# A gated recurrence with its input projection: weights loaded to all 128 partitions first, x turned in columns of four, the preamble in a new order

## The chip, the core and the metric

One core of a Trainium2 chip. The time is that of one execution on the device, in microseconds (us). TensorE is called PE here as in the profile, VectorE DVE, ScalarE ACT, GpSimd POOL; SP is the engine that only issues DMAs in this kernel. "ACTq" and "SPq" in a row are the queues from which ACT and SP issue DMAs.

## What is computed

A recurrence over 512 time steps with 512 units for a batch of 32, its inputs projected by three matrices W, its condition by three matrices C, its state by three matrices U; the input is added to the states at the end. Everything is float32.

```python
vz = video @ C_z + b_z;  vr = video @ C_r + b_r;  vh = video @ C + b       # video: (32, 512)
xz = seq @ W_z;  xr = seq @ W_r;  xh = seq @ W                             # seq = x: (32, 512, 512)
def step(h, xs):
    xzt, xrt, xht = xs
    z = sigmoid(xzt + h @ U_z + vz)
    r = sigmoid(xrt + h @ U_r + vr)
    hh = tanh(xht + r * h @ U + vh)
    h_new = (1.0 - z) * h + z * hh
    return (h_new, h_new)
result = x + all h_new, in order of time
```

## The kernel before

**Layout.** The batch has 32 rows, the partitions are 128, so a row vector of 512 numbers is laid out in J = 4 parts of 32 partitions with N = 128 columns each: partition 32 j + b holds columns 128 j to 128 j + 127 of batch row b. `part(j)` is a part's partitions, `cols(c)` a run of 128 columns. DVE's transpose turns each 32 x 32 block by itself. After it, partition 32 j + s, column 32 q + b holds number 128 j + 32 q + s of row b, and the contraction runs in Q = 4 passes q over 128 partitions. A weight matrix must have the same order of rows: partition 32 j + s, pass q holds row 128 j + 32 q + s. `load_weights` makes it so with one load for each part of 32 partitions, four to a matrix (`rows = source.rearrange("(j q s) e -> j s q e", ...)`). Parts 0 and 2 are issued by SP, 1 and 3 by ACT (`BY_QUEUE`).

**Split products.** The projections of x and the products with U_r and U_z are made of float16 parts. For this each matrix has its largest magnitude taken on DVE (`top_of_w`, line 529), summed over the partitions on PE (`total_w`, line 285), turned into a power of two on DVE (`scale_of_w`, lines 535 to 539), and split into a high half on ACT (`high_w`, line 407) and a rest on DVE (`rest_of_w`, line 546). W_r and W_z share a scale, W_h has its own, U_z and U_r share one. x goes the same way in sets of four time steps: sum of magnitudes on ACT (`sum_x`, line 382), total on PE (`total_x`, line 285), power on DVE (`power_x`, `least_x`, `up_x`), whole and high values on ACT (lines 385 and 388), rest on POOL (line 210), and at last `turn_x` (line 514), one DVE transpose for each time step, of 128 four-byte words that each hold a high and a low float16.

**Preamble.** SP and ACT issue the loads in the order in which `block` lists them: W_r, W_z, the first block of x (8 time steps), W_h, the condition, U_z, U_r, the biases, C_r, C_z, C_h, U_h, three more blocks of x. ACT waits for x before it issues its share of the C matrices and U_h. PE's order has the base products (line 255, the condition by C) behind all totals; DVE's has the bases (`bases`, lines 561 and 564) behind the rest of W_h and ahead of the rest of U_r. The first step can begin when the rests of U_r and U_z are made and x is projected for it.

**A step.** PE: the reset product h by U_r (line 303), the update product h by U_z (312), a quarter of the projection of a later time step (276), the candidate product (266), the other three quarters of the projection. DVE and ACT between them: gate_r (ACT, 432), reset and its transpose (DVE, 637 and 639), the seed of the next step's gates (518), `turn_x` for three steps ahead (514), gate_c (ACT, 441), taken (661), the new state (665), its transpose h_t (669), its high half h_hi (ACT, 428) and its rest h_lo (DVE, 611). The order within each engine is written out by hand; semaphores tie the engines together. Input blocks of 8 steps are loaded four blocks ahead.

## Time and profile before

| | |
|---|---|
| median of 3 runs | 2236.66 us (2235.65 to 2237.01) |
| profiled execution | 2234.19 us |
| its span, first to last instruction | 2232.4 us |
| PE busy | 2179.1 us (98%) |
| DVE busy | 1751.8 us (78%) |
| ACT busy | 1326.2 us (59%) |
| mean granted clock of PE | 0.999 |

The span is that of the instructions, the execution's time has a little around it. Busy time of PE is that of pipelined instructions and no measure of how well it is used. The page divides the span by engine, by line and by slices, and follows the chain that ended last; the trace can be asked for single instructions in a stretch, for groups by line and shape, and for what moved on the DMA engines in a stretch.

### The profile page before, as it was taken

The page shows a single profiled execution, that of the slowest core. Times are in us where ns is not written, and L with a number is a line of the kernel's source. Part 1 is how long each engine was busy: PE and PEld are TensorE (multiplying, and loading weights), DVE is VectorE, ACT ScalarE, POOL GpSimd, SP SyncE. Part 2 cuts the span into 40 slices and gives each one's busy share as a digit, 9 for nine tenths or more (in the row PEclk, how much of TensorE's full clock was granted, in tenths as well). Part 3 has the DMA queues.
Part 4 walks back from the last instruction along what each step waited for, and adds up shares of the span by engine and source line. Part 5 has one row for each costly group of instructions (what it writes and reads, how often), then busy time and mean ns, then how long its engine had stood idle before and what let it go on. Part 6 is the DMA issues. An engine that isn't in the chain of part 4 may idle for free.

```text
span 2232.4 us, 238869 instructions
## 1 busy us (share of the span) xinstructions
PE 2179.1 (98%) x107827; PEld 1805.7 (81%) x107827; DVE 1751.8 (78%) x8225; ACT 1326.2 (59%) x4623; POOL 689.1 (31%) x1546
## 2 busy tenths in 40 slices
PE   1899999999999999999999999999999999999999
PEld 1788888888888888888888888888888888888888
DVE  4678877877777787787777778778777777877876
ACT  3566666666666665666666566566666656656664
POOL 0233333333333333333333333333333333333332
PEclk9999999999999999999999999999999999999999
DMA  9101101101101101111111011011011011011000
GB/s 209 24 20 38 38 19 38 38 19 38 38 19 38 38 19 38 33 25 38 26 32 38 19 38 38 20 38 38 19 38 38 19 38 38 19 39 36 21 19 19
DMA packets 145138, 78.20 MB, mean 35 GB/s; under 512 B 8789, under 2 KB 140373, under 8 KB 144981
## 3 DMA queue, kind: packets, MB, share of 16 engines
q1 hardware_dynamic: 142388, 72.12, 13.4%
q10 hardware_dynamic: 2592, 4.72, 1.0%
q14 instruction: 150, 1.22, 0.2%
q8 instruction: 8, 0.13, 0.0%
HBM read 43.25 MB, written 33.55 MB: 34 GB/s over the span
## 4 chain that ended last, share of the span: by engine, by line
PE 97%; SPq 2%; DMA 1%; issue 0%; DVE 0%; ACT 0%; DVEq 0%
PE p_bank L276 45%; PE c_bank L266 21%; PE banks L303 16%; PE banks L312 15%; SPq L146 1%; DMA c_w<-in_L_cond_C_dram 1%; SPq L164 0%; PE p_bank L285 0%; DVE uz_lo L546 0%; DVE ur_lo L546 0%; SPq L154 0%; SPq L160 0%; PE c_bank L255 0%; DVE reset L637 0%; DVE h_lo L611 0%
## 5 line engine op out<-in xcount | busy, mean ns | idle before, releaser
L276 PE MATMUL p_bank<-w_hi,x_t 128*32 128x384 f16 x16480 | 1188.3, 326 | 0.0
L276 PE MATMUL p_bank<-w_lo,x_t 128*32 128x384 f16 x8240 | 706.9, 326 | 0.0
L276 PEld LDWEIGHTS p_bank<-w_hi,x_t 128*32 128x32 f16 x16480 | 470.2, 97 | 150.2 <-issue 1.5
L266 PEld LDWEIGHTS c_bank<-u,reset_t 128*32 128x32 f32 x32768 | 482.2, 110 | 96.9 <-DVE reset_t L639 95.0
L266 PE MATMUL c_bank<-u,reset_t 128*32 128x64 f32 x32768 | 551.8, 219 | 2.2 <-issue 2.2
L237 POOL TENSOR_TENSOR result<-x_nat,state 128x128 f32<-128x128 f32 x512 | 234.1, 457 | 989.2 <-DVE h_lo L611 987.4
L432 ACT ACTIVATE gate_r<-banks,gates_down 128x64 f32<-128x64 f32 x1024 | 265.6, 310 | 355.0 <-PE banks L303 341.9
L441 ACT ACTIVATE gate_c<-c_bank 128x64 f32<-128x64 f32 x1024 | 228.4, 223 | 288.5 <-PE c_bank L266 288.3
L223 POOL TENSOR_TENSOR kept<-keep,state 128x128 f32<-128x128 f32 x512 | 236.8, 463 | 520.7 <-ACT keep L435 520.7
L637 DVE TENSOR_TENSOR reset<-gate_r,state 128x64 f32<-128x64 f32 x1024 | 208.7, 204 | 205.3 <-ACT gate_r L432 199.1
L428 ACT ACTIVATE h_hi<-h_t 128x64 f16<-128x64 f32 x1024 | 260.8, 255 | 150.2 <-DVE h_t L669 83.2
L303 PE MATMUL banks<-ur_hi,h_hi 128*32 128x128 f16 x8192 | 300.5, 219 | 3.4 <-ACT h_hi L428 3.4
L303 PE MATMUL banks<-ur_hi,h_lo 128*32 128x128 f16 x8192 | 301.4, 221 | 0.0
L303 PE MATMUL banks<-ur_lo,h_hi 128*32 128x128 f16 x8192 | 300.4, 219 | 0.2 <-issue 0.2
L611 DVE SCALAR_TENSOR_TENSOR h_lo<-h_t,h_hi 128x64 f16<-128x64 f32 x1024 | 230.8, 226 | 81.6 <-ACT h_hi L428 80.7
L639 DVE STREAM_TRANSPOSE reset_t<-reset 128x64 f32<-128x64 f32 x1024 | 251.3, 245 | 35.4
L276 PEld LDWEIGHTS p_bank<-w_lo,x_t 128*32 128x32 f16 x8240 | 234.7, 97 | 48.5
L661 DVE TENSOR_TENSOR taken<-gate_c,gate_z 128x64 f32<-128x64 f32 x1024 | 226.5, 221 | 59.6 <-ACT gate_c L441 16.7
L669 DVE STREAM_TRANSPOSE h_t<-state 128x64 f32<-128x64 f32 x1024 | 247.3, 241 | 17.7
L210 POOL TENSOR_TENSOR x_parts<-x_whole,x_parts 128x128 f16<-128x128 f32 (+1 forms) x509 | 237.4, 466 | 28.0 <-ACT x_parts L388 28.0
L518 DVE SCALAR_TENSOR_TENSOR banks<-p_bank,x_down,base 128x256 f32<-128x256 f32 x512 | 236.5, 462 | 3.0 <-issue 3.0
L435 ACT ACTIVATE keep<-banks,gates_minus 128x128 f32<-128x128 f32 x512 | 188.0, 367 | 78.3 <-PE banks L312 72.9
(68 smaller groups left out, 2776.1 us busy)
## 6 DMA issues: line engine op xcount, KB each, us to landing
x_nat<-in_x_dram SPq DMA_DIRECT2D x256, 128.0 KB, 3.1
out_dram<-result SPq DMA_DIRECT2D x252, 128.0 KB, 2.8
w_stage<-in_L_cond_W_r_dram SPq DMA_DIRECT2D x2, 256.0 KB, 5.0
w_stage<-in_L_cond_W_r_dram ACTq DMA_DIRECT2D x2, 256.0 KB, 5.6
w_stage<-in_L_cond_W_z_dram SPq DMA_DIRECT2D x2, 256.0 KB, 9.0
w_stage<-in_L_cond_W_z_dram ACTq DMA_DIRECT2D x2, 256.0 KB, 9.6
w_stage<-in_L_cond_W_dram ACTq DMA_DIRECT2D x2, 256.0 KB, 11.7
u<-in_L_cond_U_z_dram ACTq DMA_DIRECT2D x2, 256.0 KB, 13.5
```

What stands on the lines that cost most here:

```text
L210: return nc.gpsimd.tensor_tensor(x_parts[k][:, part_of, 1], x_whole[k][:, part_of], x_parts[k][:, part_of, 0], ALU.subtract)
L223: nc.gpsimd.tensor_tensor(kept[:], keep[:], state[:, (tt - 1) % SLOTS], ALU.mult).then_inc(kept_ready, 1)
L237: nc.gpsimd.tensor_tensor(result[o][:, t], x_nat[j % BUFS][:, t], state[:, tt % SLOTS], ALU.add)\
L266: last = nc.tensor.matmul(c_bank[part(j), a, 0:N // HALVES], reset_t[:, part(q)], u[:, C, q, half_cols(j, a)], start=False, stop=q == Q - ...
L276: last = nc.tensor.matmul(p_bank[k][part(j), 0:G * N], x_t[:, c, part(q), a], w[b][:, :, q, cols(j)], start=f == 0, stop=f == GROUPS - 1, ...
L303: last = nc.tensor.matmul(out[part(j)], (h_hi, h_lo)[a][:, part(q)], ur[b][:, q, cols(j)], start=False, stop=n == len(passes) - 1 and q == ...
L312: last = nc.tensor.matmul(out[part(j)], (h_hi, h_lo)[a][:, part(q)], uz[b][:, q, cols(j)], start=False, stop=q == Q - 1, skip_group_check= ...
L428: nc.scalar.activation(h_hi[:, half(a)], h_t[:, half(a)], ACT.Copy, scale=2.0 ** POW)\
L432: nc.scalar.activation(gate_r[:, half(a)], banks[k][:, R, half(a)], ACT.Sigmoid, scale=gates_down[:])\
L518: V.scalar_tensor_tensor(banks[k][:, :, 0:N], p_bank[k][:, 0:GATES * N].rearrange("p (g n) -> p g n", g=GATES), x_down[d][:, W_GATES:W_GAT ...
L639: V.transpose(reset_t[:, half(a)], reset[:, half(a)]).then_inc(reset_t_ready, 1)
L669: V.transpose(h_t[:, half(a)], new[:, half(a)]).then_inc(h_t_ready, 1)
```

## The change

W and C are loaded by SP alone, each matrix with one load to all 128 partitions (`load_by_four`): partition p holds rows 4 p to 4 p + 3, which lie side by side in memory. These six loads come first, then the first block of x, then U_z, U_r and U_h by parts of 32 partitions as before, but by SP alone, then the other x blocks. ACT issues the condition and the biases, each by parts of 32 partitions: 4 + 12 loads.

With rows 4 p to 4 p + 3 on a partition, pass q must have number 128 j + 4 s + q of row b on partition 32 j + s. So `turn_x` reads its 128 words in four runs of every fourth word (`rows_of_four`) and writes them side by side (`rows_in_turn`). The condition is first copied in that order to a new tile `cond_turned` and then transposed. The base products and the projections are the same instructions on the other order of rows; the products with U are as before.

The preamble's orders change. PE: the base products stand behind the total of W_h and ahead of the totals of x. ACT: the high parts of W_r, W_z and W_h come before the sums of x. DVE: the rests of W_r and W_z come before the scales of x, the rest of W_h and the reduction of U_z behind them, then the three first turns of x, then the reduction and scale of U_r. In the very last step the second half of the new state is formed before four semaphore increments instead of behind them.

```diff
--- before.py
+++ after.py
...
@@ -33,7 +34,6 @@
     GROUPS = Q * len(PARTS)
     BEFORE_C = 3
     PE_SLOT, DVE_SLOT = 0, 8
-    BY_QUEUE = {nc.sync.engine: (0, 2), nc.scalar.engine: (1, 3)}
     POW = 14
     LEAST = 2.0 ** -60
     SETS = T // SET
@@ -85,6 +85,7 @@
         gate_r, gate_z, gate_c = sb("gate_r", [P, N]), sb("gate_z", [P, N]), sb("gate_c", [P, N])
         keep, kept, taken = sb("keep", [P, N]), sb("kept", [P, N]), sb("taken", [P, N])
         cond_nat = sb("cond_nat", [P, N])
+        cond_turned = sb("cond_turned", [P, N])
         cond_t = sb("cond_t", [P, N])
         bias = sb("bias", [P, G, N])
         base = sb("base", [P, G, N])
@@ -140,10 +141,11 @@
         def cols(c):
             return slice(N * c, N * (c + 1))
 
-        def load_weights(queue, tile, source, done):
-            rows = source.rearrange("(j q s) e -> j s q e", j=J, q=Q)
-            for p in BY_QUEUE[queue.engine]:
-                queue.dma_start(tile[part(p)], rows[p]).then_inc(done, 16)
+        def rows_of_four(tile):
+            return tile.rearrange("p (s q) -> p q s", q=Q)
+
+        def rows_in_turn(tile):
+            return tile.rearrange("p (q s) -> p q s", q=Q)
 
         block = ctx.enter_context(nc.Block())
 
@@ -153,18 +155,22 @@
                 for p in range(J):
                     sp.dma_start(x_nat[j][part(p)], x_rows[n, p]).then_inc(x_in[j], 16)
 
-            load_weights(sp, w_stage[:, R], W_r, s_w_in[R])
-            load_weights(sp, w_stage[:, Z], W_z, s_w_in[Z])
+            def load_weights(tile, source, done):
+                rows = source.rearrange("(j q s) e -> j s q e", j=J, q=Q)
+                for p in range(J):
+                    sp.dma_start(tile[part(p)], rows[p]).then_inc(done, 16)
+
+            def load_by_four(tile, source, done):
+                sp.dma_start(tile, source.rearrange("(p q) e -> p q e", q=Q)).then_inc(done, 16)
+
+            for g, m in enumerate((W_r, W_z, W_h)):
+                load_by_four(w_stage[:, g], m, s_w_in[g])
+            for g, c in enumerate((C_r, C_z, C_h)):
+                load_by_four(c_w[:, g], c, s_c_in[g])
             load_x(0, 0)
-            load_weights(sp, w_stage[:, C], W_h, s_w_in[C])
-            sp.dma_start(cond_nat[:], cond.rearrange("b (j e) -> j b e", j=J)).then_inc(s_cond_in, 16)
-            load_weights(sp, u[:, Z], U_z, s_u_in[Z])
-            load_weights(sp, u[:, R], U_r, s_u_in[R])
-            for g, b in enumerate((b_r, b_z, b_h)):
-                sp.dma_start(bias[:, g], b.rearrange("(j e) -> j e", j=J).unsqueeze(1).to_broadcast([J, B, N])).then_inc(s_bias_in, 16)
-            for g, c in enumerate((C_r, C_z, C_h)):
-                load_weights(sp, c_w[:, g], c, s_c_in[g])
-            load_weights(sp, u[:, C], U_h, s_u_in[C])
+            load_weights(u[:, Z], U_z, s_u_in[Z])
+            load_weights(u[:, R], U_r, s_u_in[R])
+            load_weights(u[:, C], U_h, s_u_in[C])
             for n in range(1, BUFS):
                 load_x(n, n)
 
@@ -321,15 +327,15 @@
             total_w(W_GATES)
             pe.wait_ge(s_w_up, W_GATES + 1)
             total_w(W_C)
+            pe.wait_ge(s_cond_t, 1)
+            for g in range(G):
+                pe.wait_ge(s_c_in[g], 16)
+                product(base_cell(g), cond_t, c_w[:, g], first=True).then_inc(s_base_mm, 1)
+            pe.wait_ge(s_w_up, W_C + 1)
             pe.wait_ge(s_row_sum, J + 1)
             for m in range(2):
                 total_x(1, m, 1 + m, m + 1)
-            pe.wait_ge(s_w_up, W_C + 1)
             total_w(U_GATES)
-            pe.wait_ge(s_cond_t, 1)
-            for g in range(G):
-                pe.wait_ge(s_c_in[g], 16 * Q)
-                product(base_cell(g), cond_t, c_w[:, g], first=True).then_inc(s_base_mm, 1)
             pe.wait_ge(s_w_up, U_GATES + 1)
             pe.wait_ge(s_zeros, 1)
             for g in range(GATES):
@@ -388,31 +394,28 @@
                 nc.scalar.activation(x_parts[m % 2][:, :, 0], set_of(m), ACT.Copy, scale=x_up[m % 2][:])\
                     .then_inc(x_hi_ready, 1)
 
-            load_weights(act, w_stage[:, R], W_r, s_w_in[R])
-            load_weights(act, w_stage[:, Z], W_z, s_w_in[Z])
-            load_weights(act, w_stage[:, C], W_h, s_w_in[C])
-            load_weights(act, u[:, Z], U_z, s_u_in[Z])
-            load_weights(act, u[:, R], U_r, s_u_in[R])
+            for p in range(J):
+                act.dma_start(cond_nat[part(p)], cond[:, cols(p)]).then_inc(s_cond_in, 16)
+            for g, b in enumerate((b_r, b_z, b_h)):
+                for p in range(J):
+                    act.dma_start(bias[part(p), g], b[cols(p)].unsqueeze(0).to_broadcast([B, N])).then_inc(s_bias_in, 16)
+
+            def high_w(g):
+                k = SCALE_OF[g]
+                act.wait_ge(s_w_up, k + 1)
+                nc.scalar.activation(split_of(g, 0), stage_of(g), ACT.Copy, scale=w_up[:, k:k + 1]).then_inc(s_w_hi, 1)
+
+            high_w(R)
+            high_w(Z)
+            high_w(C)
             act.wait_ge(x_in[0], 16 * J)
             sum_x(0, 1)
             act.wait_ge(x_summed, 1)
             sum_x(1, 2)
-            for g, c in enumerate((C_r, C_z, C_h)):
-                load_weights(act, c_w[:, g], c, s_c_in[g])
-            load_weights(act, u[:, C], U_h, s_u_in[C])
-
-            def high_w(g):
-                k = SCALE_OF[g]
-                act.wait_ge(s_w_up, k + 1)
-                nc.scalar.activation(split_of(g, 0), stage_of(g), ACT.Copy, scale=w_up[:, k:k + 1]).then_inc(s_w_hi, 1)
-
-            high_w(R)
-            high_w(Z)
             for m in range(2):
                 act.wait_ge(x_scaled, m + 1)
                 whole_x(m)
                 high_x(m)
-            high_w(C)
             high_w(UR)
             high_w(UZ)
             nc.scalar.activation(table[:], w_up[:, 0:1], ACT.Sigmoid)
@@ -511,8 +514,9 @@
 
             def turn_x(k, c, sets):
                 dve.wait_ge(x_lo_ready, sets)
-                V.transpose(x_t[:, c].rearrange("p n a -> p (n a)").bitcast(i32),
-                            x_parts[k][:, cols(c)].rearrange("p n a -> p (n a)").bitcast(i32)).then_inc(x_t_ready, 1)
+                V.transpose(rows_in_turn(x_t[:, c].rearrange("p n a -> p (n a)").bitcast(i32)),
+                            rows_of_four(x_parts[k][:, cols(c)].rearrange("p n a -> p (n a)").bitcast(i32)))\
+                    .then_inc(x_t_ready, 1)
 
             def seed_gates(k, d):
                 V.scalar_tensor_tensor(banks[k][:, :, 0:N], p_bank[k][:, 0:GATES * N].rearrange("p (g n) -> p g n", g=GATES),
@@ -525,7 +529,7 @@
                     .then_inc(c_seeded, 1)
 
             def top_of_w(g):
-                dve.wait_ge((s_u_in[Z] if g == UZ else s_u_in[R] if g == UR else s_w_in[g]), 16 * J)
+                dve.wait_ge(*((s_u_in[Z], 16 * J) if g == UZ else (s_u_in[R], 16 * J) if g == UR else (s_w_in[g], 16)))
                 V.tensor_reduce(w_top[:, g:g + 1], stage_of(g), AX.XY, ALU.max, apply_absolute_value=True)\
                     .then_inc(s_w_top, 1)
 
@@ -553,7 +557,7 @@
                 link(up_of(gates_up[:], w_pow[:, U_GATES:U_GATES + 1], 2 * POW))
                 link(V.tensor_scalar(w_down[:, W_GATES:W_GATES + 1], w_down[:, W_GATES:W_GATES + 1], gates_up[:], None,
                                      ALU.mult))
-                dve.wait_ge(s_bias_in, 16 * G)
+                dve.wait_ge(s_bias_in, 16 * J * G)
                 link(V.tensor_scalar(bias[:, 0:GATES], bias[:, 0:GATES], gates_up[:], None, ALU.mult))
 
             def bases():
@@ -567,22 +571,23 @@
             top_of_w(Z)
             scale_of_w(W_GATES)
             top_of_w(C)
-            dve.wait_ge(s_cond_in, 16)
-            V.transpose(cond_t[:], cond_nat[:]).then_inc(s_cond_t, 1)
+            dve.wait_ge(s_cond_in, 16 * J)
+            link(V.tensor_copy(rows_in_turn(cond_turned), rows_of_four(cond_nat)))
+            V.transpose(cond_t[:], cond_turned[:]).then_inc(s_cond_t, 1)
             scale_of_w(W_C)
+            rest_of_w(0)
+            rest_of_w(1)
             dve.wait_ge(x_totaled, 2)
             for m in range(2):
                 power_x(m, p_bank[1][:, G * N + m:G * N + m + 1], m, int)
                 least_x(m, m, int)
                 up_x(m, m, int)
+            rest_of_w(2)
             top_of_w(UZ)
-            top_of_w(UR)
-            rest_of_w(0)
-            scale_of_w(U_GATES)
-            rest_of_w(1)
             for c in range(TURN_AHEAD):
                 turn_x(0, c, SET)
-            rest_of_w(2)
+            top_of_w(UR)
+            scale_of_w(U_GATES)
             scales_of_gates()
             scale_down(0)
             bases()
@@ -672,12 +677,12 @@
                 renew(0)
                 take(1)
                 turn(0)
+                renew(1)
                 if last and tt == STEPS - 1:
                     dve.sem_inc(seeded, 1)
                     dve.sem_inc(c_seeded, 1)
                     dve.sem_inc(h_lo_ready, HALVES)
                     dve.sem_inc(reset_t_ready, HALVES)
-                renew(1)
                 turn(1)
 
             begin(0, 0, True)
```

## Rows read from the trace of the kernel before

**Rows 1.** Page: engines' busy time and share; the last chain by engine.

```profile
PE 2179.1 (98%) x107827; PEld 1805.7 (81%) x107827; DVE 1751.8 (78%) x8225; ACT 1326.2 (59%) x4623; POOL 689.1 (31%) x1546
...
PE 97%; SPq 2%; DMA 1%; issue 0%; DVE 0%; ACT 0%; DVEq 0%
```

**Rows 2.** Timeline to 62.5 us: start, duration (us), engine, line, operation, [idle, releaser].

```profile
4.70 0.94 ACTq L146 DMA_DIRECT2D u<-in_L_cond_U_r_dram  x2
...
12.63 2.29 DVE L529 TENSOR_REDUCE w_top<-w_stage 128x1 f32<-128x2048 f32 x1 [2.57 <-DMA w_stage<-in_L_cond_W_z_dram]
...
16.08 0.15 DVE L491 TENSOR_SCALAR w_up<-w_pow 128x1 int32<-128x1 int32 x1
...
26.09 3.89 ACT L407 ACTIVATE w_hi<-w_stage,w_up 128x2048 f16<-128x2048 f32 x2 [3.13 <-issue]
...
29.89 0.71 ACT L385 ACTIVATE x_whole<-x_nat,x_up 128x512 f32<-128x512 f32 x1
30.51 0.85 ACT L388 ACTIVATE x_parts<-x_nat,x_up 128x512 f16<-128x512 f32 x1
...
38.07 0.69 DVE L514 STREAM_TRANSPOSE x_t<-x_parts 128x128 int32<-128x128 int32 x3
...
40.91 0.15 DVE L550 COPY gates_down<-w_down 128x1 f32<-128x1 f32 x1
...
43.93 0.35 DVE L557 TENSOR_SCALAR bias<-bias,gates_up 128x256 f32<-128x256 f32 x1 [2.14 <-DMA bias<-in_L_cond_b_dram]
...
50.47 0.48 DVE L561 SCALAR_TENSOR_TENSOR base<-banks,gates_up,bias 128x256 f32<-128x256 f32 x1 [5.92 <-PE banks L255]
...
50.59 1.08 PE L255 MATMUL c_bank<-c_w,cond_t 128*32 128x128 f32 x32 [0.20 <-DMA c_w<-in_L_cond_C_dram]
...
51.94 2.34 DVE L546 SCALAR_TENSOR_TENSOR ur_lo<-u,w_up,ur_hi 128x2048 f16<-128x2048 f32 x1
...
59.98 0.23 DVE L637 TENSOR_TENSOR reset<-gate_r,state 128x64 f32<-128x64 f32 x1 [2.52 <-issue]
...
62.46 0.30 PE L303 MATMUL banks<-ur_hi,h_hi 128*32 128x128 f16 x8 [3.42 <-ACT h_hi L428]
```

**Rows 3.** By stretches: engines' busy time; then PE clock, DMA share, GB/s.

```profile
1.50:2.50 1.00, 0.00 (x0) 0.00 (x0) 0.00 (x0) 0.00 (x0) 0.71 (x4) 1.00 0.64 90
2.50:3.00 0.50, 0.00 (x0) 0.00 (x0) 0.00 (x0) 0.00 (x0) 0.26 (x2) 1.00 1.00 365
...
37.00:38.00 1.00, 0.00 (x0) 0.00 (x0) 1.00 (x1) 1.00 (x2) 0.00 (x0) 1.00 1.10 290
44.00:48.00 4.00, 1.64 (x32) 1.51 (x32) 0.51 (x2) 0.00 (x0) 0.00 (x0) 1.00 1.13 219
64.00:68.00 4.00, 4.00 (x112) 3.03 (x104) 2.65 (x15) 1.90 (x7) 0.87 (x2) 0.59 0.02 4
```

**Rows 4.** Timeline of two steps in the middle of the span.

```profile
1000.98 0.23 DVE L661 TENSOR_TENSOR taken<-gate_c,gate_z 128x64 f32<-128x64 f32 x1
...
1003.70 0.24 DVE L639 STREAM_TRANSPOSE reset_t<-reset 128x64 f32<-128x64 f32 x1
...
1003.87 0.18 DVE L637 TENSOR_TENSOR reset<-gate_r,state 128x64 f32<-128x64 f32 x1
...
1004.79 0.31 DVE L514 STREAM_TRANSPOSE x_t<-x_parts 128x128 int32<-128x128 int32 x1
...
1004.95 0.45 ACT L441 ACTIVATE gate_c<-c_bank 128x64 f32<-128x64 f32 x2 [0.56 <-PE c_bank L266]
...
1005.20 0.22 DVE L661 TENSOR_TENSOR taken<-gate_c,gate_z 128x64 f32<-128x64 f32 x1
...
1006.38 0.29 PE L303 MATMUL banks<-ur_hi,h_hi 128*32 128x128 f16 x8
```

**Rows 5.** Groups by form, DVE, 80 to 2225 us: count, busy, mean ns, idle.

```profile
L639 DVE STREAM_TRANSPOSE reset_t<-reset 128x64 f32<-128x64 f32 x1015 | 249.1, 245 | 35.1
...
L514 DVE STREAM_TRANSPOSE x_t<-x_parts 128x128 int32<-128x128 int32 x505 | 157.1, 311 | 26.2
```

More of the change, by code:

```diff
@@ L389, in high_x @@
                     .then_inc(x_hi_ready, 1)
-            load_weights(act, w_stage[:, R], W_r, s_w_in[R])
-            load_weights(act, w_stage[:, Z], W_z, s_w_in[Z])
-            load_weights(act, w_stage[:, C], W_h, s_w_in[C])
-            load_weights(act, u[:, Z], U_z, s_u_in[Z])
-            load_weights(act, u[:, R], U_r, s_u_in[R])
-            act.wait_ge(x_in[0], 16 * J)
-            sum_x(0, 1)
-            act.wait_ge(x_summed, 1)
-            sum_x(1, 2)
-            for g, c in enumerate((C_r, C_z, C_h)):
-                load_weights(act, c_w[:, g], c, s_c_in[g])
-            load_weights(act, u[:, C], U_h, s_u_in[C])
+            for p in range(J):
[3 more added lines that the diff above has]
+                    act.dma_start(bias[part(p), g], b[cols(p)].unsqueeze(0).to_broadcast([B, N])).then_inc(s_bias_in, 16)
             def high_w(g):
@@ L410, in _ @@
             high_w(Z)
+            high_w(C)
+            act.wait_ge(x_in[0], 16 * J)
+            sum_x(0, 1)
+            act.wait_ge(x_summed, 1)
+            sum_x(1, 2)
             for m in range(2):
```

## The prediction

> **What bounds the kernel now.** I read the page first. PE is busy 98% of the span, and the chain that ended last is 97% PE; the 2% of SP's queue and the 1% of a C load in it lie ahead of the first step [rows 1]. So the time has two parts: a preamble that ends with the first reset product, and 512 steps. The profiled execution took 2234.19 us around a span of 2232.4; the median of the runs shown is 2236.66. Differences are carried over to that median.
>
> The timeline of the preamble comes next. The first reset product starts at 62.46 [rows 2]. Going back: DVE starts the first step's reset at 59.98 after 2.52 us of issue; in front of that stood the rests of U_z and U_r, the latter from 51.94. That one stood behind both bases, and DVE had waited 5.92 us for the first of them. The third base product started when C_h was in, at 50.59. So the landing of the C matrices sets the end of the preamble. From the rest of U_r to the first reset product are 62.46 - 51.94 = 10.5 us, which no load of weights sets.
>
> The view by stretches says how fast loads run: 219 GB/s with the DMA engines busy all the time (share 1.13); everything loads to 32 partitions [rows 3]. Up to 2.5 us little moves (90 GB/s in that last microsecond), so in effect data flow from about 1.9.
>
> Last, one step. Steps follow each other at 4.22 us (`taken` at 1000.98 and 1005.20), and the reset product at 1006.38 shows no idle time of PE ahead of it [rows 4]. But neither is there room to see: anything that delays `taken`, state, h_t and h_hi delays PE.
>
> **The change, part by part.**
>
> *W and C first, each as one load to 128 partitions.* No row shows such a load at work. Lower bound: the 219 GB/s of now. Upper bound: the fastest stretch, 365 GB/s over half a microsecond; between them one whole microsecond shows 290 [rows 3]. I take 300, near the middle: no gain can't be excluded, and since the engines' share is already full at 219, a gain has to come from each packet getting shorter. The Trainium skill (SBUF — State Buffer, Door 1: The DMA port swizzle) has 32 partitions reach half of the 16 ports, with 189 GB/s at 1 MiB against 328 for 128 partitions; the trace shows 219 where it says 189, and by 328 the forecast would be 1.8 us lower.
>
> *Landings.* Six matrices of 1.049 MB are 6.29 MB: 21.0 us at 300 GB/s (28.7 at 219, 17.2 at 365). Condition and biases are now 16 loads of 16 KB, 0.26 MB, 1.2 us. Then the first x block (0.52 MB), U_z and U_r (2.10 MB) from SP's queue alone; I give these 207 GB/s, a little under the 219, since one queue feeds them instead of two: 12.7 us. A landing lags the mean flow, since its last packet ends it: I add 1.0 us, between nothing and 4. U_r is in at 1.9 + 21.0 + 1.2 + 12.7 + 1.0 = 37.8. Counted back from there: U_z 32.7, x 27.6, C_h 25.1. Forwards: W_r 7.6, W_z 11.1, W_h 14.6. Behind it U_h at 43, the second x block at 45.
>
> *Issues.* ACT issues 16 small loads, at 0.47 each (two in 0.94 [rows 2]) from 0.75 to about 8.3, ahead of its first work. That is the high part of W_r, not before 14.9, so 6 us cover them. SP issues 34 loads instead of 38 and does nothing else there. Nothing on the path.
>
> *Until U_r is in.* Reductions of W_r and W_z (2.29 each) end at 10.0 and 13.5; the scale is up 1.3 behind a reduction (14.92 to 16.23 [rows 2]), at 14.8. The reduction of W_h ends at 17.2. The new copy of the condition is not in the trace; a one-column operation takes 0.15, three 128-column transposes 0.69 [rows 2], so between 0.15 and 0.69; I take 0.3, the transpose another 0.3, and W_h's scale is up at 18.7. ScalarE's high parts (1.95 each, two in 3.89) run to 20.8. The rests of W_r and W_z (2.34 each) end at 23.6. Then DVE waits for x, in at 27.6: sums on ScalarE 1.7, totals and small operations 1.6, to 30.9. Rest of W_h to 33.2, reduction of U_z to 35.5, three turns of x to 36.2. U_r lands at 37.8: 1.6 us cover this whole row, the new copy too. PE's base products, now ahead of x's totals in its order, start with C_h at 25.1 and end before 29.3, when x's sums are ready; a C_h later than about 28 would hold the totals, and DVE behind them.
>
> *From U_r in to the first step.* Wake 0.1, reduction 2.28, scale 1.31; then scales of the gates 0.9 (from 40.91 now), bias and x scales 0.6 (from 43.93), bases 0.8 and the links between, 2.5 together [rows 2]. The high part of U_r on ScalarE (2.0) fits in these 2.5. The rest of U_r starts 6.2 us behind the landing, at 44.0, and from there the 10.5 of now: 54.5. Biases and bases cost no wait any more, their inputs being in since 25. The second x block (45) is wanted by ScalarE about 47, U_h (43) at the first candidate product. Against 62.46 that is 8.0 us less.
>
> *x turned in columns of four.* 512 transposes now read 4-byte words that lie 16 bytes apart. A 128-column transpose takes 311 ns, a 64-column one 245, so 1.03 ns a column [rows 5]. That of x starts at 1004.79 and `taken` at 1005.20, 0.25 behind the start of gate_c at 1004.95, which releases it [rows 4]. How early could it go? Behind a transpose that it doesn't depend on, an operation starts 0.17 after the transpose's start (1003.70, 1003.87), 0.07 ahead of its end. So `taken` could start at 1005.03, and the transpose may grow by 0.17 us before a step does. What stride costs: from below nothing; the nearest rows are ScalarE's writing every second half word, 0.85, against whole words, 0.71, over 512 columns: 0.3 ns a column, 0.04 us here [rows 2]. From above: two columns' time for each would be 0.13, three 0.26. I take the nearest row's 0.04, which costs a step nothing. The cover is those 0.17 us; beyond it, each nanosecond costs 0.5 us.
>
> *The end.* The last half state is formed ahead of some semaphore increments instead of behind them. PE runs on for one product more after the last state, and that ends the span. Nothing.
>
> **Sum:** 8.0 us less, 2228.7; I say 2228.6.
>
> **The rivals.**
>
> *A, the loads are no faster* (14%). For it: the DMA share is full already. Against: the 290 and 365 in single stretches. U_r in at 1.9 + 28.7 + 1.2 + 12.7 + 1.0 = 45.5, the first step at 62.2, 0.3 us less: 2236.4. With a lag of 4 us, 2239.4.
>
> *B, the strided turn holds each step* (13%, the other side). Place: DVE, between the gates' seed and `taken`. It decides from a transpose of 311 + 170 = 481 ns; 16 ns beyond that eat the 8 us. At three columns' time for one, 0.26 more, each step grows by 0.09, 512 steps by 46 us: 2275. For it: nothing behind `taken` has room, and at two columns' time only 0.04 is left. Against: 0.3 ns a column on ScalarE. The page of the Trainium skill named above, in the same section, says that each SBUF access to a new line of 16 bytes pays a penalty; here every read is one, it gives no size, and no row shows it.
>
> *C, the loads run at 365* (inside the forecast's 70%). U_r in at 34.0, or 33.0 without a lag; the first step at 49.7, 12.8 less: 2223.9. DVE would then be through with the turns of x at about 32.4, so it is nearly the bound, and still shorter loads would give less.
>
> *D, the entry grows* (3%): the 2.52 of issue before the first reset, or the slow clock (0.59 of full at 64:68, so partly the level of 1.2 GHz) that PE was granted after it had stood idle [rows 2, 3]. Each is worth 1 to 3 us.
>
> **Numbers.** 70% for the forecast, whose own range is 2223 to 2233. A's bound with its lag carries the range to 2239, C's carries it to 2223; B is left out. A difference of 0.2% (4.5 us) is about what a measurement of this kernel can tell from none. Faster 0.71, same 0.16 (A, D, and the forecast's upper edge), slower 0.13 (B).
>
> **What would show it.** Right: first reset product near 54.5, U_r's reduction near 37.8 after a short idle time, some 300 GB/s from 3 to 24 us, base products at 25 and PE waiting for x behind them, steps of 4.22, x's transpose under 0.48 us with `taken` still released by gate_c. Wrong: 219 GB/s in the first 20 us (A); a transpose over 0.48 and longer steps (B); DVE without idle time ahead of U_r's reduction (C and beyond).

## The result, and the profile after

The changed kernel takes 2220.48 us (median of 4 runs, 2219.81 to 2220.98) against 2236.15 for the kernel before, run beside it (4 runs, 2234.22 to 2237.01): ratio 0.9933 (95% interval 0.9922 to 0.9945), 15.7 us less. The forecast was 8.0 us less, 2228.6, and its range began at 2223: the sign was right, the size only half of what was measured. In the experiments below the kernel before had medians of 2234.94 to 2235.68 over 13 to 25 runs, so its median of four, 2236.15, is on the high side, and the gain lies between 14.5 and 15.7 us.

The profiled execution took 2220.79 us, its span 2219.0, 13.4 less than the 2232.4 of before. The other 2 us are no work of the change that a trace shows: the profiled execution of before was 2 us faster than the median of its kernel. The page, against [rows 1]:

```profile
PE 2180.7 (98%) x107827; PEld 1808.6 (82%) x107827; DVE 1803.3 (81%) x8226; ACT 1328.9 (60%) x4623; POOL 692.7 (31%) x1546
...
PE 98%; SPq 1%; DMA 1%; issue 0%; DVE 0%; ACT 0%; DVEq 0%
```

PE has the same work. DVE has 51.5 us more, and nothing on the page says yet whether any engine waits for it. SP's queue has 1% of the chain in place of 2%, which points at the preamble. Its timeline, against [rows 2]:

```profile
5.74 2.29 DVE L533 TENSOR_REDUCE w_top<-w_stage 128x1 f32<-128x2048 f32 x1 [5.74 <-DMA w_stage<-in_L_cond_W_r_dram]
8.65 2.29 DVE L533 TENSOR_REDUCE w_top<-w_stage 128x1 f32<-128x2048 f32 x1 [0.62 <-DMA w_stage<-in_L_cond_W_z_dram]
...
14.56 0.26 DVE L575 COPY cond_turned<-cond_nat 128x128 f32<-128x128 f32 x1
...
20.15 1.08 PE L261 MATMUL c_bank<-c_w,cond_t 128*32 128x128 f32 x32 [1.34 <-DMA c_w<-in_L_cond_C_dram]
...
28.53 2.29 DVE L533 TENSOR_REDUCE w_top<-u 128x1 f32<-128x2048 f32 x1 [0.52 <-DMA u<-in_L_cond_U_z_dram]
30.73 0.96 DVE L517 STREAM_TRANSPOSE x_t<-x_parts 128x128 int32<-128x128 int32 x3
33.25 2.29 DVE L533 TENSOR_REDUCE w_top<-u 128x1 f32<-128x2048 f32 x1 [1.55 <-DMA u<-in_L_cond_U_r_dram]
...
38.91 2.34 DVE L550 SCALAR_TENSOR_TENSOR ur_lo<-u,w_up,ur_hi 128x2048 f16<-128x2048 f32 x1
...
42.13 0.39 ACT L431 ACTIVATE h_hi<-h_t 128x64 f16<-128x64 f32 x2
43.02 2.34 DVE L550 SCALAR_TENSOR_TENSOR uz_lo<-u,w_up,uz_hi 128x2048 f16<-128x2048 f32 x1
...
45.78 0.40 DVE L642 TENSOR_TENSOR reset<-gate_r,state 128x64 f32<-128x64 f32 x1 [0.42 <-issue]
...
48.52 0.29 PE L309 MATMUL banks<-ur_hi,h_hi 128*32 128x128 f16 x8 [1.64 <-ACT h_hi L431]
```

The first reset product stands at 48.52 and not 62.46: 13.9 us earlier. From there to the end of the span it is 2170.5 us, before 2169.9. So the whole gain lies ahead of the first reset product, and the order in it is the forecast's: reductions as the matrices land, base products done early, and U_r's reduction waiting last for a load, 1.55 us (1.6 were forecast). But U_r is in at 33.2, not 37.8. The rate tells why, by stretches as in [rows 3] (the last three columns are PE clock, DMA share and GB/s):

```profile
3.00:8.00 5.00, 0.00 (x0) 0.00 (x0) 2.26 (x1) 0.00 (x0) 0.39 (x2) 1.00 1.02 415
8.00:13.00 5.00, 0.39 (x16) 0.34 (x16) 3.64 (x8) 1.99 (x2) 0.00 (x0) 1.00 1.01 386
13.00:18.00 5.00, 3.06 (x60) 2.46 (x64) 4.83 (x9) 5.00 (x3) 0.00 (x0) 1.00 1.03 412
...
26.00:42.00 16.00, 5.56 (x79) 2.89 (x83) 12.74 (x21) 7.32 (x7) 2.16 (x1) 0.50 1.13 213
44.00:48.00 4.00, 2.21 (x56) 1.66 (x56) 3.47 (x11) 1.24 (x4) 2.10 (x2) 1.00 0.05 11
```

W and C came at 404 GB/s on average (the first three rows); from 26 to 42 us, with U and later blocks of x, the rate was 213. The DMA engines' share is full in both: what differs is what a full share moves. The steps, against [rows 4] and [rows 5] (first a stretch of the timeline, then the groups of DVE by form from 80 to 2215 us, with idle time last):

```profile
1003.99 0.42 DVE L517 STREAM_TRANSPOSE x_t<-x_parts 128x128 int32<-128x128 int32 x1
...
1004.14 0.45 ACT L444 ACTIVATE gate_c<-c_bank 128x64 f32<-128x64 f32 x2 [0.55 <-PE c_bank L272]
...
1004.40 0.23 DVE L666 TENSOR_TENSOR taken<-gate_c,gate_z 128x64 f32<-128x64 f32 x1
...
1005.58 0.29 PE L309 MATMUL banks<-ur_hi,h_hi 128*32 128x128 f16 x8
```

```profile
L666 DVE TENSOR_TENSOR taken<-gate_c,gate_z 128x64 f32<-128x64 f32 x1010 | 223.4, 221 | 5.9 <-ACT gate_c L444 1.9
L517 DVE STREAM_TRANSPOSE x_t<-x_parts 128x128 int32<-128x128 int32 x502 | 214.3, 427 | 26.8
```

The strided turn takes 427 ns and not 311, yet `taken` starts 0.26 us behind gate_c's start, as before (0.25). The idle time ahead of `taken` shrank to 5.9 us over 1010 of them; before it was this:

```profile
L661 DVE TENSOR_TENSOR taken<-gate_c,gate_z 128x64 f32<-128x64 f32 x1014 | 224.3, 221 | 56.5 <-ACT gate_c L441 13.8
```

The turns of x grew by 58 us in this stretch (over the same number of them), and the wait ahead of `taken` shrank by 51: most of the growth went into time in which DVE had waited.

### The profile page after: what moved, and what is told of

It is laid out like the page before. It is cut to its first block, busy times and chain, and to the rows that moved or that the text cites. A ratio compares the mean times of both kernels' runs of the same rounds, so it can differ in the third digit from the quotient of the medians.

```text
span 2219.0 us, 238863 instructions
## 1 busy us (share of the span) xinstructions
PE 2180.7 (98%) x107827; PEld 1808.6 (82%) x107827; DVE 1803.3 (81%) x8226; ACT 1328.9 (60%) x4623; POOL 692.7 (31%) x1546
## 4 chain that ended last, share of the span: by engine, by line
PE 98%; SPq 1%; DMA 1%; issue 0%; DVE 0%; ACT 0%; DVEq 0%
PE p_bank L282 45%; PE c_bank L272 21%; PE banks L309 16%; PE banks L318 15%; DMA u<-in_L_cond_U_r_dram 1%; SPq L156 0%; SPq L161 0%; PE p_bank L291 0%; SPq L164 0%; DVE w_top L533 0%; DVE uz_lo L550 0%; ACT uz_hi L406 0%; ACT L421 0%; DVE reset L642 0%; PE banks L291 0%
## 5 line engine op out<-in xcount | busy, mean ns | idle before, releaser
L517 DVE STREAM_TRANSPOSE x_t<-x_parts 128x128 int32<-128x128 int32 x512 | 218.2, 426 | 28.5 <-POOL kept L229 1.4
```

## The experiments

Behind each run's median stands the median of the kernel before, run beside it, and their ratio with its 95% interval. The baselines differ by up to 1.2 us (2234.94 to 2236.15), so a difference of less than that between two changed kernels of different batches is not safe. The table has every kernel without an operation added to the steps: start of U_r's reduction and of the first reset product in the profiled execution, the median of the timed runs, and what the median exceeds the first product by. For the kernel before it has the profiled execution in place of the median.

| kernel | U_r reduced from | first product | median, us | median less first product |
|---|---|---|---|---|
| before (profiled execution) | | 62.46 | 2234.19 | 2171.7 |
| changed | 33.25 | 48.52 | 2220.48 | 2172.0 |
| e1_w32 | 46.59 | 62.09 | 2234.36 | 2172.3 |
| e2_w128_2k | 37.77 | 53.11 | 2224.49 | 2171.4 |
| e3_turn_plain | 33.57 | 48.76 | 2219.94 | 2171.2 |
| e4_base_late | 32.36 | 49.28 | 2221.95 | 2172.7 |
| f1_before_halves | | 63.09 | 2237.69 | 2174.6 |
| f2_u_halves | 33.11 | 48.33 | 2223.88 | 2175.6 |
| h1_small_as_one | 38.41 | 54.17 | 2227.33 | 2173.2 |
| h2_mixed | 42.39 | 57.61 | 2230.01 | 2172.4 |
| h3_c_last | 26.58 | 47.92 | 2220.63 | 2172.7 |
| h4_c_last_table | 26.72 | 48.23 | 2221.08 | 2172.9 |

Ten of the twelve rows lie within 2171.2 to 2173.2 while the first product moves by 14 us: the time follows the first product. In the other two more is lost behind it (see f1 and f2). The first product has a scatter of its own: in g1, whose preamble is that of the kernel before, it stands at 60.23 and not 62.46, with C_h used from 48.28 and not 50.59.

**e1_w32: width taken back.** W and C go by four loads to 32 partitions each, 8 KB side by side still; all else of the change stays.

```diff
-                sp.dma_start(tile, source.rearrange("(p q) e -> p q e", q=Q)).then_inc(done, 16)
+                rows = source.rearrange("(p q) e -> p q e", q=Q)
+                for p in range(J):
+                    sp.dma_start(tile[part(p)], rows[part(p)]).then_inc(done, 16)
```

> The changed kernel, but each W and C matrix is loaded by four loads of 32 partitions, still in rows of four (8 KB side by side per partition). Theory: the width of a load sets its rate; the six matrices fall back to some 220 GB/s, take 28 us instead of 15.5, U_r is in near 46 instead of 33.2, the first reset product starts near 61 and the time is near 2233. Rival: the longer pieces (8 KB instead of 2 KB) made the rate; then this run is within 1 us of the changed kernel, 2220.5, with packets of 8 KB still at 0.31 us.

**e2_w128_2k: width kept, pieces of 2 KB.** The same two lines, but four loads to all 128 partitions, `sp.dma_start(tile[:, q], rows[:, q])`.

> The changed kernel, but each W and C matrix is loaded by four loads, one for each pass, each to 128 partitions in pieces of 2 KB. Theory (width): the rate stays near 400 GB/s, U_r is in near 33, the time is 2220.5 within 1 us. Rival (piece length): some 220 GB/s, U_r in near 46, 2233. Halfway, about 300 GB/s, U_r near 39, 2226, would mean that both count.

e1 took 2234.36 against 2234.96, 0.9997 [0.9987, 1.0006], and e2 2224.49, 0.9952 [0.9935, 0.9968]. The stretches of e1, then of e2:

```profile
3.00:8.00 5.00, 0.00 (x0) 0.00 (x0) 0.00 (x0) 0.00 (x0) 0.39 (x2) 1.00 1.03 214
8.00:13.00 5.00, 0.00 (x0) 0.00 (x0) 2.29 (x1) 1.28 (x1) 0.00 (x0) 1.00 1.03 212
```

```profile
3.00:8.00 5.00, 0.00 (x0) 0.00 (x0) 0.00 (x0) 0.00 (x0) 0.39 (x2) 1.00 0.90 246
8.00:13.00 5.00, 0.00 (x0) 0.00 (x0) 3.16 (x2) 1.28 (x1) 0.00 (x0) 1.00 1.04 371
13.00:18.00 5.00, 0.39 (x16) 0.34 (x16) 4.26 (x7) 2.23 (x2) 0.00 (x0) 1.00 1.05 379
```

With 32 partitions to a load the share is as full and the rate is half, and nothing of the gain is left: long pieces, x turned in fours, the new order of the preamble and the split small loads together bring nothing measurable (by the interval, from 2.9 us less to 1.3 more). Together with e2, which has as many issues as e1 and keeps the width, this shows width to be the cause. With 2 KB pieces on 128 partitions the steady rate is 375, 6% under that of the changed kernel (399 over the same ten microseconds); only the first stretch is far below (246 against 415), with the share at 0.90. Which of the two made it slow there, the pieces or four issues in place of one, was not separated. The mean over 3 to 18 us is 332 and U_r's reduction began at 37.8, by coincidence the moment that the forecast had named for the changed kernel.

**e3_turn_plain: x turned without stride.** x's columns then meet rows of W in another order, so the projections compute something else.

```diff
-                V.transpose(rows_in_turn(x_t[:, c].rearrange("p n a -> p (n a)").bitcast(i32)),
-                            rows_of_four(x_parts[k][:, cols(c)].rearrange("p n a -> p (n a)").bitcast(i32)))\
+                V.transpose(x_t[:, c].rearrange("p n a -> p (n a)").bitcast(i32),
+                            x_parts[k][:, cols(c)].rearrange("p n a -> p (n a)").bitcast(i32))\
```

> The changed kernel with the transposes of x reading their 128 words side by side as before; the projections then meet the rows of W in another order, which is a change of what is computed. The transpose should fall from 0.43 to 0.31 us. Theory: the 0.12 us are covered, steps stay at 4.22 us and the time is 2220.5 within 1 us. Rival: the covered time was smaller than I read and each step pays some of it; then this run is faster, by 0.5 us for each nanosecond that a step paid.

2219.94 against 2234.96, 0.9931 [0.9915, 0.9948]: 0.5 us below the changed kernel, and the ranges of the two overlap.

```profile
L666 DVE TENSOR_TENSOR taken<-gate_c,gate_z 128x64 f32<-128x64 f32 x1010 | 223.8, 222 | 55.7 <-ACT gate_c L444 13.0
...
L517 DVE STREAM_TRANSPOSE x_t<-x_parts 128x128 int32<-128x128 int32 x502 | 156.3, 311 | 25.7
```

The turn is 311 ns again, the wait ahead of `taken` is back, and the time does not move measurably. The stride costs 0.116 us a turn, 59 us in all, of which at most about 0.5 is seen in the time.

**g1_before_plus and g2_after_plus: how much cover there is.** A transpose of 64 columns that nobody reads stands behind x's turn in each step, in the kernel before and in the changed one.

```diff
+        spare = sb("spare", [P, N // 2])
...
+                    V.transpose(spare[:], reset[:, half(0)])
```

> The kernel before plus one 64-column transpose to an unused tile behind the transpose of x in every step. An operation behind it can start 0.17 us later than without it. I read 0.17 us of cover there, so by the theory a step pays 0 to 0.01 us, the time is up by 0 to 6 us. Rival (there is more cover, or DVE's time there doesn't matter): 0; rival (less cover, 0.1): 0.07 us a step, 36 us.

> The changed kernel plus the same unused transpose. The strided transpose of x has taken 0.12 of the 0.17 us of cover, so by the theory a step now pays 0.17 - 0.05 = 0.12 us: 60 us more, 2280, with steps of 4.34 us. Rival (the strided reads cost nothing because there is far more cover): within 5 us of 2220.5.

g1 took 2239.05 against 2234.94, 1.0020 [1.0010, 1.0030], and g2 2233.73, 0.9998 [0.9988, 1.0007], which is 13 us above the changed kernel. One turn in g1, then in g2:

```profile
1001.05 0.31 DVE L515 STREAM_TRANSPOSE x_t<-x_parts 128x128 int32<-128x128 int32 x1
1001.29 0.20 DVE L657 STREAM_TRANSPOSE spare<-reset 128x64 f32<-128x64 f32 x1
1001.46 0.22 DVE L663 TENSOR_TENSOR taken<-gate_c,gate_z 128x64 f32<-128x64 f32 x1
...
1001.21 0.45 ACT L442 ACTIVATE gate_c<-c_bank 128x64 f32<-128x64 f32 x2 [0.56 <-PE c_bank L267]
```

```profile
1000.87 0.42 DVE L518 STREAM_TRANSPOSE x_t<-x_parts 128x128 int32<-128x128 int32 x1
1001.22 0.20 DVE L662 STREAM_TRANSPOSE spare<-reset 128x64 f32<-128x64 f32 x1
1001.34 0.18 DVE L668 TENSOR_TENSOR taken<-gate_c,gate_z 128x64 f32<-128x64 f32 x1
...
1001.02 0.45 ACT L445 ACTIVATE gate_c<-c_bank 128x64 f32<-128x64 f32 x2 [0.55 <-PE c_bank L273]
```

In g1 `taken` still starts 0.25 behind gate_c: the spare transpose takes just the 0.17 us of cover. The starts of the 512 seeds of the gates on DVE place the time of g1. Its first product came 2.2 us sooner than in the profiled execution of before, and its steps took 6.1 us more: 1.4 in the first steps, 3.2 spread over the 448 steps of the program's loop (0.007 a step; about half of it at the ends of the loop's seven passes of 64 steps), and 1.5 in one wait called issue ahead of a `state` at 1972.80, soon after the loop is left.

In g2 `taken` starts 0.32 behind gate_c, 0.07 late, and a step takes 4.247 us in place of 4.226: some 0.05 of the 0.07 is taken up behind `taken`. That is 9 of the 13 us; 2 more lie at the ends of the seven passes, and the same wait as in g1, 1.48 here, has the rest. The last 64 steps, which the program writes out behind the loop, are the control. There x's turn starts 0.24 us ahead of gate_c and not 0.15, `taken` starts 0.26 behind gate_c with the spare transpose in place, and from the wait to the last seed a step takes 4.225 us in all four kernels (before, changed, g1, g2). So what g2 pays in each step is there where `taken` is late and gone where it is not. I had expected 60, holding that nothing behind `taken` has room.

**e4_base_late: base products behind the totals.** The four lines with the waits for the turned condition and for C, and `product(base_cell(g), ...)`, move in PE's order behind the totals of x and U.

> The changed kernel with PE's base products put back behind the totals of x and of U_z and U_r. Theory: they then start when the reduction of U_r is through (36) and take 3.6 us or, at the lower clock, 5; bases and projections slip by about 3 us, the first reset product from 48.5 to 51.5, the time from 2220.5 to 2223.5. Rival: the landing of U_r alone sets the start and PE's order is free: 2220.5.

2221.95 against 2234.96, 0.9941 [0.9924, 0.9957]: 1.5 us above the changed kernel, half of what was expected. The products begin at 34.93, as U_r's total is out, and at 38.33, and U_r's rest starts at 40.33 and not 38.91:

```profile
34.93 3.62 PE L261 MATMUL banks<-c_w,cond_t 128*32 128x128 f32 x64
38.33 1.72 PE L261 MATMUL c_bank<-c_w,cond_t 128*32 128x128 f32 x32
...
40.33 2.34 DVE L550 SCALAR_TENSOR_TENSOR ur_lo<-u,w_up,ur_hi 128x2048 f16<-128x2048 f32 x1
```

U_r's reduction began 0.9 us sooner here than in the changed kernel, so what the order alone is worth is not sharper than this: 1.5 to 2.0 us (the latter against e3, run beside it), of 15.7.

**f1_before_halves: the kernel before, each queue with neighbouring partitions.** One line; the theory was that two queues at work on different quarters of SBUF are as good as width.

```diff
-    BY_QUEUE = {nc.sync.engine: (0, 2), nc.scalar.engine: (1, 3)}
+    BY_QUEUE = {nc.sync.engine: (0, 1), nc.scalar.engine: (2, 3)}
```

> The kernel before with one line changed: SP issues the loads to partitions 0 to 63 (parts 0 and 1) and ACT those to partitions 64 to 127 (parts 2 and 3), instead of parts 0 and 2 by SP and 1 and 3 by ACT. Order, sizes and pieces stay. Theory: what counts is that both halves of the partitions are written at the same time; before, parts 0 and 1 (the same half) went together and then 2 and 3. Then the rate rises from 219 towards the 332 GB/s that loads of 2 KB pieces to 128 partitions had, C_h is in near 38 instead of 50.6, and the time falls by about 9 us to 2226. Rival: only a load that spans all partitions is fast; then 219 GB/s and no change, 2235.

2237.69 against 2234.94, 1.0015 [1.0005, 1.0024]. The nine microseconds did not come.

```profile
3.00:8.00 5.00, 0.00 (x0) 0.00 (x0) 1.42 (x1) 1.28 (x1) 0.38 (x2) 1.00 1.06 340
8.00:13.00 5.00, 0.40 (x16) 0.34 (x16) 3.29 (x3) 0.00 (x0) 0.00 (x0) 1.00 1.10 281
13.00:18.00 5.00, 0.00 (x0) 0.00 (x0) 0.53 (x5) 0.00 (x0) 0.00 (x0) 1.00 1.13 210
```

Assigning the halves did raise the rate, to 340 from 227, for the first 5 us; by 13 us it had gone. Why is open. A gain seen in the first stretch was no gain in the end: C_h was used from 50.21, 0.4 us sooner than before, the first reset waited 3.52 us of issue in place of 2.52, and the steps right behind it took 2.6 us more in sum.

**f2_u_halves: the same for U in the changed kernel.** SP loads two quarters of each U, and ScalarE's queue the other two, once C_h is in.

```diff
+            act.wait_ge(s_c_in[C], 16)
+            for g, m in ((Z, U_z), (R, U_r), (C, U_h)):
+                rows = m.rearrange("(j q s) e -> j s q e", j=J, q=Q)
+                for p in range(J // 2, J):
+                    act.dma_start(u[part(p), g], rows[p]).then_inc(s_u_in[g], 16)
```

> The changed kernel, with parts 2 and 3 of the three U matrices issued by ACT as soon as C_h is in, and parts 0 and 1 by SP as before. Theory (both halves at once): from 20 us on some 300 GB/s instead of 220, U_r in near 29 instead of 33.2; then DVE, with the rest of W_h, U_z and the turns of x in front, starts U_r's reduction near 31; the first reset product 2 us earlier, 2218.5. Rival (only whole loads are fast): no change in the rate; the time is 2220.5, or up to 2 us more for ACT's 2.7 us of issues ahead of the sums of x.

2223.88 against 2234.94, 0.9953 [0.9937, 0.9970]. The rate rises to 290 from 24 to 30 us, U_r's reduction starts 0.14 sooner and has no wait ahead of it any more: DVE is the bound there. The median is 3.4 us above the changed kernel's. About half of that lies outside the span: the four executions took 2.1 to 3.8 us more than their spans, those of the changed kernel 1.8. The other half lies in the spans (median 2220.5 against 2218.7), in the profiled one as 0.003 us a step of the loop. Both halves are unexplained.

**h1_small_as_one: condition and biases each as one load again**, now with the four parts outermost; the first of its two changes:

```diff
-            for p in range(J):
-                act.dma_start(cond_nat[part(p)], cond[:, cols(p)]).then_inc(s_cond_in, 16)
+            act.dma_start(cond_nat[:], cond.rearrange("b (j e) -> j b e", j=J)).then_inc(s_cond_in, 16)
```

> The changed kernel with the condition and the three biases loaded as before, one load each with the four parts as outermost dimension (four loads of 64 KB, now issued by ACT), instead of 16 loads of 16 KB. Theory: such a load runs on only four of the DMA engines, so these four carry 48 KB more than the others, in 512-byte packets of about 0.05 us or 5 us of work, and every landing, which needs its slowest engine, comes 3 to 5 us later: U_r in at 37, the time near 2224. Rival: the small loads spread over all engines either way: 2220.5.

2227.33 against 2235.68, 0.9966 [0.9954, 0.9979]: 6.8 us above the changed kernel, with W and C still at 399 GB/s from 3 to 18 us. C_h, and behind it x and both U, land late:

```profile
22.61 1.93 PE L261 MATMUL c_bank<-c_w,cond_t 128*32 128x128 f32 x32 [2.78 <-DMA c_w<-in_L_cond_C_dram]
34.15 2.28 DVE L531 TENSOR_REDUCE w_top<-u 128x1 f32<-128x2048 f32 x1
38.41 2.29 DVE L531 TENSOR_REDUCE w_top<-u 128x1 f32<-128x2048 f32 x1 [1.10 <-DMA u<-in_L_cond_U_r_dram]
```

0.26 MB in this form hold up all that lies behind them, U_r by 5.2 us. The mean flow from 3 to 18 us does not show it. I read it so: these loads lie on few of the DMA engines, and each landing behind them waits for the slowest. That is argued, not shown; that the form costs 6.8 us is shown. (The Trainium skill, page "DMA: Bandwidth & Descriptors", section "Why a DMA increments its semaphore by 16", says that a transfer's slowest dimension, if it isn't 1, sets how many engines share it: the largest number up to 16 that divides it on both sides; with four parts outermost that is four. This run agrees in its result, and does not show the engines one by one.) Splitting the small loads is the second half of the gain.

**h2_mixed: narrow loads beside wide ones.** U_z and U_r are issued by ScalarE's queue from the start, ahead of condition and biases.

> The changed kernel, but U_z and U_r (32 partitions to a load) are issued by ACT at the very start, beside SP's W and C loads to 128 partitions. Theory: in the mix each DMA engine serves both queues in turn, so the rate from 3 to 18 us lies between 220 and 400 (near 280), W_r and W_z land a little later, U_r lands at about 20, but the first x block only near 29; DVE's order waits for x first, so the first reset product comes about 4 us later, 2224. Rival, that the mix costs the wide loads more than their turns (the narrow loads hold ports that the wide ones need): below 250 GB/s and W_z in after 14, over 2226.

2230.01 against 2235.68, 0.9977 [0.9967, 0.9986]. From 3 to 24 us the rate was 355, 340, 339 and 336 in turn, not the 280 expected: keeping the kinds apart is worth less than I thought. The loss has another place. The condition stood behind U in ScalarE's queue, so the base products began only at about 31 us, with x's totals behind them on PE; U_r's reduction started at 42.39.

**h3_c_last and h4_c_last_table: U ahead of C.** C's loads go behind U_r, the base products between x's totals and U's; h4 also loads the sigmoid table ahead of U_r's high part.

```diff
-            for g, c in enumerate((C_r, C_z, C_h)):
-                load_by_four(c_w[:, g], c, s_c_in[g])
...
+            for g, c in enumerate((C_r, C_z, C_h)):
+                load_by_four(c_w[:, g], c, s_c_in[g])
```

> The changed kernel with the three C loads behind U_r instead of ahead of x, and PE's base products behind the totals of x, ahead of that of U_r. Theory: U_r is in near 26 instead of 33.2 since 3.15 MB (7.8 us at 404 GB/s) no longer stand ahead of it; then DVE is the bound, which works from 5.8 on without a wait: U_r's reduction from about 27 to 29.5, base products held by C_h (30), the rest of U_r near 34 instead of 38.9; the first reset product near 43.5, 2215.5. Rival: a C load late again holds the bases, as in the kernel before: no gain or a loss, 2220 or more.

> The one before with ACT's sigmoid table loaded ahead of the high part of U_r, while ACT waits, instead of behind that of U_z. Theory: h_hi no longer stands behind 1.5 us of table work, and DVE's wait of 0.5 us for it goes: 0.5 us less, 2215.0. Rival: no difference, since DVE or PE holds it there.

2220.63 and 2221.08 against 2235.68: 0.9935 [0.9918, 0.9951] and 0.9937 [0.9920, 0.9953]. U_r's reduction starts 6.7 and 6.5 us sooner than in the changed kernel, and all is lost again. h3:

```profile
26.58 2.25 DVE L533 TENSOR_REDUCE w_top<-u 128x1 f32<-128x2048 f32 x1
...
32.04 1.93 PE L261 MATMUL c_bank<-c_w,cond_t 128*32 128x128 f32 x32 [0.85 <-DMA c_w<-in_L_cond_C_dram]
...
37.06 2.35 DVE L550 SCALAR_TENSOR_TENSOR ur_lo<-u,w_up,ur_hi 128x2048 f16<-128x2048 f32 x1
...
45.35 0.22 DVE L642 TENSOR_TENSOR reset<-gate_r,state 128x64 f32<-128x64 f32 x1 [1.84 <-issue]
```

C_h, now last, holds PE until 34, and U's total stands behind it: 4.8 of the 6.7 us go there. The reset, 1.85 us ahead by then, comes 0.4 sooner: the wait called issue is 1.84 in place of 0.42. In h4 it is 2.65, and the reset stands at 45.66. In the changed kernel, e4, f2, h3 and h4 the first reset comes between 45.35 and 46.04, whatever came earlier. No row of the timeline names what holds DVE there.

The view of the DMA queues shows one thing beside it. Besides the loads there are queues that it calls "instruction". In all 14 profiled kernels a packet of the one called q14 moves 2.0 to 2.5 us ahead of the first reset, whatever time DVE was ready: at 43.7 in the changed kernel, 42.9 in h3, 43.2 in h4, 57.7 in the kernel before (only h2 has another one in between). The first reset is the first operation inside the program's loop. So the wait may be for instructions of the loop; no run here tests it.

## Why the prediction was wrong in size

**The step that failed: 300 GB/s for W and C, with 365 as upper bound.** Measured: 404. 6.29 MB then take 15.6 us and not 21.0. C_h landed 5.0 us sooner than forecast and, the 12.7 us behind it being 13.1, U_r 4.5: these are 4.5 of the 5.9 us missed ahead of the first reset product. In all 7.7 us were missed: these 5.9, and 2.0 and 0.3 by which medians and profiled executions differ, less 0.5 that the steps gave back. The 365 was no bound: it was half a microsecond of loads of the old kind [rows 3]. Rival C, which used it, named the right direction and still came out 3.4 us long. The page of the Trainium skill cited in the prediction ("SBUF — State Buffer", Door 1) gives 189 GB/s to 32 partitions and 328 to 128 for a transfer of 1 MiB, and 218 and 436 as what longer flow comes near. The runs here show 214 (e1), 375 in steady flow for 2 KB pieces (e2) and 404 for 8 KB: with loads queued behind each other the second pair is the nearer one, and the forecast took only the first. No row of before showed a wide load, and the share, full at 219 already [rows 3], could not tell how much a full share can move.

**The small loads.** In their new form the price of 1.2 us, by their bytes, held: with the measured rate the forecast's sum gives 1.9 + 15.6 + 1.2 + 1.0 = 19.7 for C_h, and it was in at 20.1. In the form that they had before they cost 6.8 us beside fast loads (h1). The forecast named no gain from the split; its lag of up to 4 us for a landing is the only place where such a cost could stand. Width and the split don't simply add up: without width the split and all else are worth nothing (e1); without the split, width brings 8.4 us (2235.68 less 2227.33).

**From U_r in to the first product: 16.7 forecast, 15.3 measured.** 0.5 us lie ahead of the rest of U_r (5.66 against 6.2), 0.9 behind it. The 2.52 of issue ahead of the first reset shrank to 0.42, a gain of 2.1; 1.2 of it went again, 0.9 of that ahead of the reset, where DVE now waited 0.54 us for h_hi behind ScalarE's table and 0.20 for PE's projection at half clock. Rival D had this place and only its growth in mind.

**The slow clock moved.** PE was granted 0.59 in the first step before [rows 3]; now it is granted 0.50 (its level of 1.2 GHz) from 26 to 42 us, where it works 5.6 of 16 us, and 1.00 from 44. The first step is 4.28 us long and not 5.93 (first reset product to first of the next). The gain of 1.65 was paid back: PE's waits called issue in the next steps sum to 5.0 us in place of 3.3. What they wait for is open.

**x turned in fours: nothing per step, rightly; the size of the cost wrongly.** The nearest row gave 0.04 us for the stride, measured 0.116 (e3 against the changed kernel), 0.9 ns for each 4-byte word at 16 bytes' distance. Cover of 0.17 was right (g1 fills it without a delay); the strided turn uses two thirds. "Nothing behind `taken` has room" was wrong: about 0.05 us has (g2), so for these 70 ns beyond the cover a nanosecond costs 0.15 us over 512 steps, not 0.5. Rival B's point of decision, 481 ns, was not reached; rival A is refuted by the rate.

**Nothing on the path** held for the condition's copy (0.26, in the range of 0.15 to 0.69), the issues and the end (2170.5 us behind the first product against 2169.9).

**The carry-over to the median** added 2 us of error: differences were taken against the profiled execution, 2 us below the median, and set off from the median.

**Open:** why f1's rate fell after 10 us, why f2's executions are longer than the landing of U_r promises, what the waits called issue in the first steps and behind the loop (g1, g2) are for, whether the first reset waits for the instructions of the loop, and which DMA engines carried the small loads of h1.

## What to carry to other kernels

Give a bulk load all 128 partitions: it moved nearly twice as much at the same DMA share here, and a full share in a profile says nothing of bytes. Look for the small loads in front of the large ones: their form, not their bytes, can hold up each landing behind them. An upper bound taken from rows of the old kind of transfer is no bound for a new kind; and ahead of a loop, ask what else stands at its entry before a sooner landing is counted as gain.

## What the hardware showed that was not expected

- Wide loads move 404 GB/s (386 to 415 in stretches of 5 us), narrow ones 204 to 243 (e1 and the kernel before, stretches of 5 or 6 us), at the same full share; narrow and wide mixed in two queues still move 336 to 355 (h2).
- Two queues with half of the partitions each moved 340 for 5 us, and 210 from 13 us on (f1).
- A transpose of 128 words of 4 bytes takes 427 ns when the words that it reads lie 16 bytes apart, 311 ns when they lie side by side.
- At the entry to the steps DVE waits 0.2 to 3.5 us and PE, over the first steps, 3.3 (before) and 5.0 us (changed) for nothing that the timeline names. In the changed kernel, h3 and h4 DVE's wait grows by about what is saved ahead of it (0.42, 1.84, 2.65).
- In 14 of 14 kernels a packet of a DMA queue for instructions moves 2.0 to 2.5 us ahead of DVE's first operation in the loop.
- The same steps have 0.09 us more cover written out than in the loop: x's turn starts 0.24 us ahead of gate_c there, and 0.15 in the loop (g2).
